# A transformer, test-time-training and transformer kernel: the middle stage rewritten with an open state, 64-wide inverses and two sequences side by side

## What is computed

```python
x = x + 0.5 * ffn(layernorm(x))     # two transformer layers: local attention and MLP
x = x + attn(layernorm(x))          # the middle stage
x = x + 0.5 * ffn(layernorm(x))     # the same two layers again

def attn(x):                        # cut; DS = 64, D = 256, S = 512, rate 0.01
    h = layernorm(x) * gamma + beta
    k, v, q = h @ Wk.T + bk, h @ Wv.T + bv, h @ Wq.T + bq
    def step(W, (q_t, k_t, v_t)):   # W starts at zero, one (D, DS) matrix per sequence
        y_t = W @ q_t
        W = W - rate * outer(W @ k_t - v_t, k_t)
        return W, y_t
    return x + scan(step, ...)
```

## Time and profile before

| | us |
|---|---|
| median of three runs | 2956.71 |
| profiled execution | 2956.4 |
| its span, first to last instruction | 2954.6 |
| first transformer's last W2 product ends | 1304.6 |
| second transformer's first matmul starts | 1672.8 |

### The profile page before, as it was taken

The page is one execution under the profiler, slowest core; times in us unless marked ns, Lnnn a source line. Parts: engine busy times, 40 slices in busy tenths (PEclk is TensorE's granted clock), DMA queues, the critical chain, the costliest instruction groups (busy, mean ns, idle before and its releaser), DMA issues.

```text
span 2954.6 us, 62913 instructions
## 1 busy us (share of the span) xinstructions
PE 2831.5 (96%) x21552; PEld 2417.5 (82%) x21552; DVE 2224.6 (75%) x6568; ACT 1592.4 (54%) x4242; POOL 1390.6 (47%) x1467
## 2 busy tenths in 40 slices
PE   7999999999999999968888899999999999999998
PEld 6888888888888888857766678888888888888887
DVE  7888888877777777756677577777777777777775
ACT  5566656556666656631111266566665556655654
POOL 4455454455555445422332244555555445445543
PEclk9999999999999999989999999999999999999999
DMA  2122110011000000030000000000001100000000
GB/s 97 41 73 69 51 30 23 18 66 52 2 2 2 2 2 2 25 111 15 29 14 29 25 2 2 2 2 2 2 2 51 55 20 16 16 16 16 16 16 23
DMA packets 76859, 76.51 MB, mean 26 GB/s; under 512 B 37648, under 2 KB 63760, under 8 KB 75408
## 3 DMA queue, kind: packets, MB, share of 16 engines
q1 hardware_dynamic: 70784, 71.15, 7.5%
q10 hardware_dynamic: 5776, 1.56, 0.2%
HBM read 48.32 MB, written 23.59 MB: 24 GB/s over the span
## 4 chain that ended last, share of the span: by engine, by line
PE 74%; DVE 13%; issue 6%; ACT 5%; POOL 1%; DMA 0%; DVEq 0%; ACTq 0%; POOLq 0%; SPq 0%
PE bank L890 12%; PE bank L892 11%; PE bank L891 11%; PE bank L1080 10%; PE bank L950 6%; PE bank L980 6%; PE bank L966 5%; ACT pr L720 4%; PE bank L926 3%; DVE t L1273 2%; PE bank L1011 2%; PE bank L1211 1%; PE bank L1199 1%; DVE t L1276 1%; PE bank L1208 1%
## 5 line engine op out<-in xcount | busy, mean ns | idle before, releaser
L585 POOL TENSOR_TENSOR pr<-pr,rden 128x512 f32<-128x512 f32 (+1 forms) x512 | 469.6, 938 | 977.4 <-DVE rden L1313 973.5
L720 ACT ACTIVATE pr<-pr,nb 128x256 f32<-128x256 f32 (+1 forms) x1024 | 479.0, 469 | 271.7 <-DVE nb L1304 268.8
L1080 PE MATMUL bank<-w,uT 128*128 128x256 f32 (+1 forms) x1536 | 434.2, 398 | 0.0
L1304 DVE CUSTOM_DVE_ANT_0 pr<-bank,maskb,r 128x256 f32<-128x256 f32 (+1 forms) x1024 | 402.0, 446 | 31.0 <-PE bank L950 20.0
L890 PE MATMUL bank<-h2T,w 128*128 128x256 f32 x1408 | 405.8, 288 | 3.8
L891 PE MATMUL bank<-h2T,w 128*128 128x256 f32 x1408 | 395.0, 281 | 0.0
L892 PE MATMUL bank<-h2T,w 128*128 128x256 f32 x1408 | 394.8, 280 | 0.0
L1374 DVE SCALAR_TENSOR_TENSOR uT<-bank,b,gg 128x256 f32<-128x256 f32 (+1 forms) x384 | 182.4, 481 | 241.9 <-ACT gg L780 148.7
L890 PE MATMUL bank<-wqkv,hT 128*128 128x512 f32 x768 | 327.9, 427 | 8.0 <-DVE nb L1304 5.8
L891 PE MATMUL bank<-wqkv,hT 128*128 128x512 f32 x768 | 304.7, 397 | 0.0
L892 PE MATMUL bank<-wqkv,hT 128*128 128x512 f32 x768 | 303.2, 395 | 0.0
(11 more groups left out here) (210 smaller groups left out, 6282.2 us busy)
## 6 DMA issues: line engine op xcount, KB each, us to landing
wqkv<-wqkv_split SPq DMA_DIRECT2D x18, 512.0 KB, 6.2
w<-w_split SPq DMA_DIRECT2D x3, 2816.0 KB, 9.7
Y<-in_x SPq DMA_DIRECT2D x8, 512.0 KB, 8.3
uT<-in_x SPq DMA_DIRECT2D x8, 512.0 KB, 4.4
out<-Y SPq DMA_DIRECT2D x8, 512.0 KB, 3.4
stt<-stt SPq DMA_DIRECT2D x224, 3.0 KB
h<-out SPq DMA_DIRECT2D x7, 512.0 KB, 4.0
out<-h SPq DMA_DIRECT2D x7, 512.0 KB, 2.9
```

The lines of the kernel that those rows point to most:

```text
L585: e.tensor_tensor(pr[:, 2 * j:2 * j + 2, 0:wide], pr[:, 2 * j:2 * j + 2, 0:wide], rden[:, 2 * j:2 * j + 2].unsqueeze(2).to_broadcast([P, 2 ...
L720: last = e.activation(pr[:, hd, 0:wide], pr[:, hd, 0:wide], ACT.Exp, bias=nb[:, hd:hd + 1], scale=-1.0, accum_out=den[:, hd:hd + 1])
L1080: mm = e.matmul(bank[bk][:, 0:D], uT[0:rows, t // 2, mt, (t % 2) * P:(t % 2 + 1) * P], w2[0:rows, mt, :], start=(mt == 0), stop=(mt == MT ...
L1304: m = e.tensor_tensor_reduce(pr[:, hd, 0:wide], bank[j][:, g * 256:g * 256 + wide], far, r[:, t, 1, place(hd):place(hd) + 1], FAR, ALU.add ...
```

## The change

The hardware loop goes; the four pairs are unrolled. For each pair:

- Both sequences' keys (and queries) lie in one tile: sequence 0 in partitions 0 to 63, sequence 1 in 64 to 127 (`kqT`). Products that read them use the two row halves or two column halves of the array, one per sequence.
- The inverse is built for the two 64-wide diagonal blocks of each chunk, five levels; a level's product is eight 64x64 matmuls (`blocks`), the upper block in rows and columns 0 to 63 and the lower in 64 to 127. The first level's operands come ready from the masks. The quadrant between the blocks is joined afterwards.
- The inverse is applied to values and keys at once (`errors`), for all chunks, before any state is known. From this come per-chunk step matrices (`steps`), and the state of a chunk is then one product with the state before (`kept`) added in PSUM to the chunk's own part (`learned`); the answers likewise (`inside`, `carried`).
- Mixing and statistics are made two pairs ahead, the normalised input and its transposes one pair ahead; both normalisations are applied from one set of statistics on ScalarE as scale and bias. The output normalisation of a pair is made during the next pair, and of the last pair in the second transformer's first two sequences. The first pair's mixing, normalisation and transposes go into the last sequence of the first transformer, and the loads of x with them.

Cut to its core. Each engine's other new helpers (`mid_h`, `mid_xz`, `out_norm`, `out_stats`, `mid_rstd`) do what the list above says.

```diff
@@ SyncE
+    def mid_entry(L, b):
+        stats_moved(L, b)
+        e.wait_ge(kt_ps, at(kt_ps, idx(L, b, NT - 1) + 1))
+        e.wait_ge(qt_ps, at(qt_ps, idx(L, b, NT - 1) + 1))
+        load_mid(0, 0)
+        load_mid(0, 1)
+        e.wait_ge(pv_ps, at(pv_ps, idx(L, b, NT - 1) + 1))
+        e.dma_start(mid, A["mid"]).then_inc(T_W, 16)
+        load_mid(1, 0)
+    def mid_stage():
+        e.wait_ge(h2t_ps, at(h2t_ps, 16 * DEPTH))
+        load_mid(1, 1)
+        load_w2(DEPTH)
+        for p in range(B // 2):
+            if p + 2 < B // 2:
+                e.wait_ge(t_xz, at(t_xz, 2 * p + 2))
+                for i in pair:
+                    load_mid(p + 2, i)
+            e.wait_ge(t_y, at(t_y, 4 * p + 4))
+            for i in pair:
+                e.dma_start(x_out[:, 2 * p + i, :, :], Y[:, NT * (2 * p + i):NT * (2 * p + i + 1), :]).then_inc(t_stored[p % 2][i], 16)
@@ GpSimd, ScalarE
+    def mid_rstd(p, i):
+        k = 2 * p + i
+        e.wait_ge(t_va, at(t_va, k + 1))
+        if p:
+            e.wait_ge(t_xz, at(t_xz, k - 1))
+        e.tensor_tensor(rs1[:, i, :, :], va1[:, i, :, :], small[:, 0:1].unsqueeze(1).to_broadcast([P, 2, NT]), ALU.pow).then_inc(t_rs, 1)
+        e.wait_ge(t_rs, at(t_rs, 2 * k + 1))
+        e.tensor_tensor(off1[:, i, :, :], rs1[:, i, :, :], over_tiles(neg1[:, i, :], 2), ALU.mult)
...
+        for l in range(LV + 1):
+            for i in pair:
+                rows = ROWS[1] if l == LV else slice(0, P)
+                e.wait_ge(t_p_ps[i], at(t_p_ps[i], (LV + 1) * p + l + 1))
+                e.activation(mx[i][rows, :, :].rearrange("p c k -> p (c k)"), bank[LP_BANK[i]][rows, 0:256], ACT.Copy).then_inc(t_p[i], 1)
+            if more and l in (3, 4):
+                mid_zT(p + 1, l - 3)
...
+            e.wait_ge(t_i_ps[i], at(t_i_ps[i], TI * p + TI))
+            e.activation(wholeT[i][0:64, :, 64:P], cut(bank[LUT_BANK[i]][0:64, 0:256], NT), ACT.Copy, scale=-1.0).then_inc(t_q[i], 1)
+        def state_read(c):
+            e.wait_ge(t_s_ps, at(t_s_ps, 3 * p + c))
+            e.activation(state[:, c - 1, :], bank[STATE_BANK[c - 1]][:, 0:D], ACT.Copy).then_inc(t_s, 1)
...
+                n, w = 2 * c + i, D + DS if c else D
+                e.wait_ge(t_tv_ps, at(t_tv_ps, 8 * p + n + 1))
+                e.activation(err[i][:, c, 0:w], bank[ERR_BANK[n % 4]][:, 0:w], ACT.Copy, scale=TTT_LR).then_inc(t_tv, 1)
+                if n == 4:
+                    state_read(1)
+        state_read(2)
+        state_read(3)
+        for i in pair:
+            if p:
+                for t in range(NT):
+                    out_norm(p - 1, i, t)
+        if more:
+            for i in pair:
+                mid_xz(p + 1, i)
@@ TensorE
+    def mid_zT(p, i):
+        e.wait_ge(t_h[i], at(t_h[i], p + 1))
+        for k in range(KT):
+            if i:
+                e.wait_ge(t_zt[0], at(t_zt[0], 2 * p + k + 1))
+            elif p:
+                e.wait_ge(t_v[1], at(t_v[1], 2 * p - 1 + k))
+            else:
+                e.wait_ge(u_done, at(u_done, 12 * (B - 1) + 96 * (DEPTH - 1) + 8 + k + 1))
+            for t in range(NT):
+                m = e.transpose(bank[k][:, t * P:(t + 1) * P], hn[i][:, t, k * P:(k + 1) * P], ident[:, :])
+            m.then_inc(t_zt_ps[i], 1)
...
+        for f in range(2):
             for k in range(KT):
...
+                for i in pair:
+                    m = e.matmul(bank[KQ_BANK[f]][ROWS[i], :], tw[:, k, f * DS:(f + 1) * DS], z_T[i][:, k, :],
+                                 start=(k == 0), stop=(k == KT - 1), skip_group_check=True)
+            m.then_inc(t_kq_ps, 1)
+        mid_v(p, 0)
+        e.wait_ge(t_kq, at(t_kq, 2 * p + 1))
+        for c in range(NT):
+            m = e.transpose(bank[KQ_BANK[0]][:, c * P:(c + 1) * P], kqT[:, 0, c * P:(c + 1) * P], ident[:, :])
+        m.then_inc(t_kn_ps, 1)
+        if p:
+            e.wait_ge(t_y, at(t_y, 4 * p - 2))
+        for c in range(NT):
+            for half in range(2):
+                for i in pair:
+                    lo, hi = c * P + 64 * half, (c + 1) * P
+                    m = e.matmul(bank[KK_BANK[i]][ROWS[half], c * P:c * P + hi - lo], kqT[ROWS[i], 0, lo:lo + 64], kqT[ROWS[i], 0, lo:hi],
+                                 start=True, stop=True)
+        m.then_inc(t_kk_ps, 1)
+        e.wait_ge(t_kq, at(t_kq, 2 * p + 2))
+        if p:
+            e.wait_ge(t_y, at(t_y, 4 * p - 1))
+        for c in range(NT):
+            for i in pair:
+                m = e.matmul(bank[A_BANK[i]][:, c * P:(c + 1) * P], kqT[ROWS[i], 0, c * P:(c + 1) * P], kqT[ROWS[i], 1, c * P:(c + 1) * P],
+                             start=True, stop=True)
+        m.then_inc(t_a_ps, 1)
+        mid_v(p, 1)
+    def blocks(bk, lo, left, right):
+        for c in range(NT):
+            for half in range(2):
+                m = e.matmul(bank[bk][ROWS[half], lo + 64 * c:lo + 64 * c + 64], left[ROWS[half], c, 0:64], right[ROWS[half], c, 0:64],
+                             start=True, stop=True)
+        return m
+    def mid_levels(p):
         for l in range(LV):
             for i in pair:
                 if l == 0:
+                    e.wait_ge(t_v[0], at(t_v[0], 2 * p + i + 1))
+                else:
+                    e.wait_ge(t_m[i], at(t_m[i], (LV - 1) * p + l))
+                e.wait_ge(t_i[i], at(t_i[i], TI * p + (2 * l if l else 1)))
+                blocks(LP_BANK[i], 0, m_up[i][l % 2] if l else m_first[i], inv[i]).then_inc(t_p_ps[i], 1)
             for i in pair:
+                e.wait_ge(t_p[i], at(t_p[i], (LV + 1) * p + l + 1))
+                e.wait_ge(t_i[i], at(t_i[i], TI * p + 2 * l + 1))
                 if l == 0:
+                    e.wait_ge(t_g[i], at(t_g[i], 2 * p + 2))
+                    e.wait_ge(t_qd[i], at(t_qd[i], p + 1))
+                blocks(LU_BANK[i], 0, invT[i], mx[i]).then_inc(t_i_ps[i], 1)
+                if l == 0:
+                    e.wait_ge(t_a[i], at(t_a[i], p + 1))
+                blocks(LUT_BANK[i], 0, mx[i], invT[i]).then_inc(t_i_ps[i], 1)
+            if p + 1 < B // 2 and l in (2, 3):
+                mid_zT(p + 1, l - 2)
+        for i in pair:
+            e.wait_ge(t_i[i], at(t_i[i], TI * p + 2 * LV))
+            for c in range(NT):
+                m = e.matmul(bank[LP_BANK[i]][64:P, 64 * c:64 * c + 64], n_quad[i][0:64, c, :], inv[i][0:64, c, :], start=True, stop=True)
...
+                m = e.matmul(bank[LUT_BANK[i]][0:64, 64 * c:64 * c + 64], mx[i][64:P, c, :], wholeT[i][64:P, c, 64:P], start=True, stop=True)
...
+        def errors(c):
...
+                e.matmul(bank[ERR_BANK[n % 4]][:, 0:w], wholeT[i][:, c, :], vk[i][:, c, 0:w], start=True, stop=True).then_inc(t_tv_ps, 1)
...
+        def steps(c):
+            e.wait_ge(t_tv, at(t_tv, 8 * p + 2 * c + 2))
+            if c < NT - 1:
+                for i in pair:
+                    e.matmul(bank[STEP_BANK][ROWS[i], (c - 1) * DS:c * DS], err[i][:, c, D:D + DS], vk[i][:, c, D:D + DS], start=True, stop=True)
             for i in pair:
+                m = e.matmul(bank[STEP_BANK][ROWS[i], c * P:(c + 1) * P], err[i][:, c, D:D + DS], a_up[i][:, c, :], start=True, stop=True)
...
+        def learned(c):
             for i in pair:
+                m = e.matmul(bank[STATE_BANK[c]][ROWS[i], 0:D], vk[i][:, c, D:D + DS], err[i][:, c, 0:D], start=True, stop=(c == 0), skip_group_check=True)
...
+        def kept(c):
+            e.wait_ge(t_s, at(t_s, 3 * p + c))
             for i in pair:
+                m = e.matmul(bank[STATE_BANK[c]][ROWS[i], 0:D], step[ROWS[i], (c - 1) * DS:c * DS], state[ROWS[i], c - 1, :], start=False, stop=True, skip_group_check=True)
...
+        def inside(c):
+            for i in pair:
+                e.matmul(answer(c, i), a_up[i][:, c, :], err[i][:, c, 0:D], start=True, stop=(c == 0), skip_group_check=True)
+        def carried(c):
+            e.wait_ge(t_s, at(t_s, 3 * p + c))
+            for i in pair:
+                m = e.matmul(answer(c, i), step[ROWS[i], c * P:(c + 1) * P], state[ROWS[i], c - 1, :], start=False, stop=True, skip_group_check=True)
+                if c % 2:
+                    m.then_inc(t_y_ps, 1)
...
+        errors(0)
+        errors(1)
+        e.wait_ge(t_tv, at(t_tv, 8 * p + 2))
+        learned(0)
+        errors(2)
+        steps(1)
+        errors(3)
+        steps(2)
+        steps(3)
+        if more:
+            e.wait_ge(t_zt[1], at(t_zt[1], 2 * p + 3))
+        learned(1)
+        inside(0)
+        e.wait_ge(t_ag, at(t_ag, 2 * p + 2))
+        kept(1)
+        inside(1)
+        carried(1)
+        learned(2)
+        kept(2)
+        if more:
+            e.wait_ge(t_zt[1], at(t_zt[1], 2 * p + 4))
+        inside(2)
+        carried(2)
+        inside(3)
+        carried(3)
@@ VectorE
+    def mid_masks(p):
+        e.wait_ge(t_kk_ps, at(t_kk_ps, p + 1))
         for i in pair:
+            kk = cut(bank[KK_BANK[i]][:, :], NT)[:, :, 0:64]
```

(40 more changed lines are left out.)

655 lines of the change are left out of this document (308 added, 347 removed).

## The result

The changed kernel takes 2786.26 us, the median of four runs (2785.72 to 2787.39). The kernel before took 2955.92 beside it (2954.74 to 2956.92). The ratio is 0.9427, 95% interval 0.9410 to 0.9443. The prediction said 2798.5 with a range of 2772 to 2850: 12.2 us too slow, and inside the range. The profiled execution took 2787.4 us against 2956.4 before, 169.0 less, where 157.9 were predicted.

The account below looks back on a forecast made before the run. PE bounds the levels between the transformers, with idle waits at entry and exit. Keys at 1309.1 + pairs 201.9 + exit 1.9 + statistics 2 = 1514.9 against 1672.8, 157.9 us gained: 2956.4 becomes 2798.5, range 2772 to 2850.

Parts of the forecast that it names:

- Price of a quarter instruction: Inversion levels: 0.031 us per 64x64 quarter instruction if quarters overlap as halves do, with 0.057 kept for the range.
- Keys stage: Projections and key and query products of one pair: 13.1 us on PE, masks and copies hidden beside it.
- Memory stage: Inverse applied, steps, state and answers of one pair: 12.0 us, plus 0.9 of PE waiting for ACT's last error copy.
- Changes of shape: PE switching between matmul shapes: 26 switches per pair at 0.17 us, 4.4 us a pair.
- A pair: Keys 13.1, levels 20.5, memory stage 12.9 and switches 4.4: 50.9 us; four pairs 201.9, the last without transposes.
- Entry: End of the first transformer: pair 0's preparation moves in there, so keys begin at 1309.1, not 1327.2.
- between 0 and 4; I take 2: Second transformer's first two sequences: cost in us of the last pair's output statistics moving in.
- Loop instructions at nothing: Middle stage: removing loop instructions and extra semaphore steps gains nothing, since PE's queue covers them.
- Rival 1: Inversion levels: quarters do not overlap, a group costs 0.9 us, a pair 61.8, the time 2842; chance 0.25.
- Rival 2: Inversion levels: the clock falls in each pair, levels and joining 38.5 us, the time 2870; chance 0.10.
- Rival 3: Inversion levels: small matmuls on two quarters wait for each other, a group 3.5 us, time about 3160; chance 0.02.
- Rival 4: Inversion levels: a handover binds them, 4.2 us a level instead of 3.25, time 2818; chance 0.13.

Follow-up runs that it names:

- experiment 8: Changed kernel with the memory stage's products reordered, 10 changes of shape a pair in place of 15 (part of the third tile's answer is left out): 2785.39 us.
- experiment 12: Changed kernel with the edits of Experiment 6 and experiment 7 and most of experiment 8's order, 12 changes of shape a pair in place of 15: 2783.25 us.
- experiment 1: Changed kernel with each inversion group's four upper-row quarter products issued first, then the four lower ones, instead of taking turns: 2799.96 us.
- experiment 2: Changed kernel with key and query projections of the two sequences issued one after the other instead of in turn: 2786.35 us.
- experiment 10: Changed kernel with the inversion-level group that updates the transposed inverse issued twice: 2803.34 us.
- experiment 11: The changed kernel once more, without any edit, as yardstick: 2787.26 us.
- Experiment 6: Changed kernel with the first transformer's last W2 products issued before the second sequence's transposes: 2783.06 us.
- experiment 7: Changed kernel with 40 idle transposes of the identity where PE waits in the second transformer's first steps: 2786.02 us.
- experiment 4: Kernel before the change, with its middle stage's hardware loops written out as Python loops on every engine: 2955.63 us beside 2954.36.
- experiment 9: Changed kernel with both quarter products of each inversion pair reading operands from the upper 64 rows: 2786.79 us.
- Experiment 3: Changed kernel with each next pair's transposes and ScalarE's reads moved out of the levels to the head of that pair's keys: 2807.78 us.

## Why the prediction held, point by point

- **Price of a quarter instruction: right.** 0.0292 us measured, 0.031 taken. The level is 3.04 us in place of 3.25, the whole level stage with transposes and joining 19.99 in place of 20.5. The late starts in a level are 0.24 us, where 0.25 of waiting were taken.
- **Keys stage: 13.44 us, 13.1 predicted without changes of shape.** The 32 key products took 1.02 us (1368.75 to 1369.77), not 1.5, and a change of shape is in the 1.02: alone, 16 of 64 columns at 0.0575 and 16 of 128 at 0.109 would be 2.7 (0.109 is the transposes' price in the prediction), so more than two of the four quarters work at once. That hid the five changes of shape that stand in this stage.
- **Memory stage:** 15.13 us; the prediction's 12.9 and 15 changes of shape at 0.17 are 15.45. In the 12.9 were 0.9 us of waiting for ACT's last error copy. This step failed: PE is idle 0.04 us in the whole stage. Changes at 0.19 instead of 0.17 and some late starts brought about 0.5 of it back.
- **Changes of shape: price and count bear out.** Experiments 8 and 12 give 0.19 and 0.18 us each for the 15 of the memory stage, 0.17 was taken. The 11 others of "I count 26 such switches per pair" were not changed by an experiment, but their starts show them. From the group at 1383.19 to the transposes it is 0.57 us instead of 0.467, and the eight transposes take 1.02 up to the next group instead of 8 x 0.109 = 0.87. The query products take 1.09 instead of 16 x 0.057 = 0.91, and the second values 3.66 instead of 16 x 0.216 = 3.46. That is 0.1 to 0.2 us each.
- **A pair: 48.57 us, 50.9 predicted.** The 2.3 us are in the main three terms: five levels at 3.04 instead of 3.25 (1.0), the wait for the error copy that was not there (0.9), and the key products (0.5). In the last pair the difference is 3.2, since the changes of shape around the transposes that it does not have were left in its sum. From the keys at 1312.5 to the start of the last product at 1504.1 it is 191.6 us instead of 201.9. DVE's 34 us a pair were 31 in pair 1, and ACT's 26 were 23 to 27, without effect on the time.
- **Entry: keys at 1312.5, not 1309.1.** 1.4 us were there before the entry began (the first W2 group starts at 1294.18, in the kernel before at 1292.74). "The last W2 matmuls, 3.0 us" took 4.64, which is 1.7 more, most of it at a clock of 0.50. What is left, 0.3, is ACT's second normalisation: it stood idle 4.31 us for POOL and ended at 1305.4, not 1303.1. The step had the wait for ACT and not the clock. The entry's own 2.28 us of waiting had gone before the fall, but they alone do not decide it. Of the ten profiles with this wait, six show the clock at 0.50 in the second transposes or the last W2 group and four (experiments 1, 2, 10 and 11) do not. What decides it stays open. Experiment 6 shows the entry without the wait.
- **Exit: 1.8 us from the last product, 1.9 predicted.**
- **Second transformer: "between 0 and 4; I take 2" was wrong in sign.** From restart to end it takes 1279.6 us, 2.1 less than the 1281.8 before. The output statistics that moved in cost nothing that shows. The range of the forecast had named the cause for the other side, a clock that no longer falls: it is low for 6.8 us after the restart now. The kernel before has two such stretches there:

```profile
1671.50:1678.40 6.90, 4.65 (x11) 3.43 (x12) 2.79 (x9) 0.98 (x2) 0.98 (x1) 0.51 0.40 115
1685.20:1692.00 6.80, 6.61 (x33) 5.75 (x34) 3.18 (x22) 3.78 (x17) 2.45 (x4) 0.50 0.00 0
```

  The ninth instruction of the transposes of `Y` (L902 there) starts 52.25 us after the restart in the kernel before, 50.22 in the changed one and 49.07 with no low stretch (experiment 7). So the first 50 us hold 2.0 us of gain, and one low stretch less is the likely cause, at a price near that of experiment 7. It is not a sure one: the first of the two stretches is there in five of the ten unchanged restarts, and in the second profile of the changed kernel the clock is low there for 3.4 us more (51.4 us up to that instruction). The 2 us that were expected for the output statistics are the term that failed; nothing of them shows.
- **Loop instructions at nothing: right** (experiment 4).
- **The balance:** 157.9 predicted, less 3.4 at the entry, plus 10.3 for the pairs, 0.1 for the exit and 4.1 for the second transformer: 169.0.
- **Rival 1** fell: quarters overlap, in one bank. The rule of the Trainium skill that was set beside it ("TensorEngine Tiling (Array Packing)", "Gotcha 1: PSUM Pressure") would have given 0.9 us a group. Here two quarters with different contraction rows and results on different partitions of one bank ran at 0.467, and with the same rows too (experiment 9). The measurement decides, for this case.
- **Rival 2** fell: the granted clock is 1.00 in every stage of the pairs. But its mechanism exists one step further off. Experiment 3 made the idle time, and the clock fell behind each seam. **Rival 3** fell with rival 1. **Rival 4** fell by the level itself, 3.04 us and not 4.2, and by experiment 10.
- **Luck:** the entry was 3.4 us too early in the forecast and the second transformer and the pairs too slow, so the errors partly cancel. The 1.4 us before the entry and the clock at both ends vary from one execution to the next by as much as these terms.

## What to carry to other kernels

Small products whose results lie on different partitions can share the array in pairs, even in one PSUM bank: take a neighbouring row's series, halve it, and then look for what else takes the time, such as 0.18 us for a change of shape. Group products of one shape where the dependencies leave a choice, but do not start a second sum in a bank while a first one there still wants its other part. When preparing work ahead, follow the queue of the engine that reads it, since its backlog cost some 6 us here, as much as the clock that fell in the wait.

## What had not been expected of the hardware

- PE finds a partner for a half product beyond its next neighbour: 3.64 us instead of 3.58 with four instructions of one half in a row, 0.575 us a group instead of 0.467 with eight. In experiment 1 the first instruction of a group starts at 1382.78, ahead of the last three of the group before it (1382.83, 1382.89 and 1382.95).
- The contraction rows do not matter for it where the results lie on different partitions (experiment 9), and with four quarters in use 32 products took 1.02 us.
- A stretch at half clock costs at most half of the PE work that falls into it. In experiment 3, 5.1 of its 10.3 us fell into the keys and lengthened them by 2.5; at the restart PE was busy for 5.40 of the 6.8 us, and they cost 1.2 to 1.5.
- Idle transposes where PE waits kept the clock up at the restart and did not delay the steps behind them: the first scores start 11.05 us after the restart with them and 11.04 without. They gave 1.2 to 1.5 us there and 5.2 over three seams.
